# Attention denominators inverted in place and spread over partitions through DRAM, in a new instruction order

## The chip, the cores and the metric

The kernel runs on one core of a Trainium2 chip, as one launch. The core's engines run side by side, each through its own instruction queue in order, and meet at semaphores: TensorE (PE, matmul), VectorE (DVE), ScalarE (ACT), GpSimd (POOL) and SyncE (SP), which here only issues DMAs. SBUF is the on-chip memory, PSUM holds matmul results, DRAM is off chip. The metric is device time in microseconds (us), lower is better.

## What is computed

For x of 4 x 2048 rows of 256 numbers the kernel computes `x + s * silu(g)`, where both branches read the same layer norm xn of x. Cut to what matters here, per batch b, with 16 heads of 64:

```
Q = elu(xn @ Wq + bq) + 1;  K = elu(xn @ Wk + bk) + 1;  v = xn @ Wv + bv
KV = einsum('bshd,bshm->bhdm', K, v)
Z = 1 / (einsum('bshd,bhd->bsh', Q, K.sum(axis=1)) + 1e-6)
o = einsum('bshd,bhdm,bsh->bshm', Q, KV, Z);   attn_out = o @ Wo + bo
x1 = layer_norm(xn + attn_out);  s = layer_norm(x1 + gelu(x1 @ W1 + b1) @ W2 + b2)
g = fp4_linear(silu(fp4_linear(xn, w_gate)) * fp4_linear(xn, w_up), w_down)
```

`fp4_linear` rounds both operands in blocks of 16 to a grid of 4-bit numbers before it multiplies. All is float32; a product is made of three matmuls on a high and a low part of each operand (`mm3`, lines 74 to 77).

## The kernel before

The rows are 64 tiles of 128 (`NT`), in 16 groups of 512 rows (`NG`). A first stage, up to about 520 us, makes the layer norm, the K sums (`ksB`) and, for each batch, the maps `Mh`, `Ml` = KV times Wo. The second stage, which the change concerns, goes through the groups. Nothing is scheduled automatically: for each engine the order is written out by hand, a loop over groups whose body lists steps of this group and of the ones around it. Each step first waits on semaphores. In a group the tiles are a, b, c, d.

The steps that the text below speaks of:

- `q_proj(g,j)` (PE, 6 matmuls of 512 columns into the bank QH), `q_exp` (ACT) and `q_elu` (DVE, L1584) make Q for two heads at a time, j = 0 to 7, as `Q32[:, j, :]` with features on the partitions and 512 rows in the free dimension.
- The denominators. `den_sums` (PE, L676) multiplies `ksB` with Q: 8 matmuls of 512 columns, four of which write different 32-partition strips of the bank AC. `den_copy` (ACT, L1169) takes them to `dn_s`, `den_turn` (PE, L685) transposes them, `den_inverse` (DVE, L1715 to L1723) adds 1e-6, inverts and splits into a high and a low part, `z_turn` (PE, L692) transposes back, `z_copy` (ACT, L1174) stores `zs`, and eight `z_spread` (PE, L704) copy one row of `zs` to the 64 partitions of its head with a selecting matrix `sel`, into QH.
- `z_mul(g,j)` (DVE, L1729) multiplies `Q32[:, j, :]`, in SBUF, with the bank in PSUM that `z_spread` wrote. `z_hi` (ACT, L1088) and `z_lo` (DVE, L1738) split the product, and `at_step(g,j)` (PE, 12 matmuls of 256 columns into AC) adds its part to the attention output.
- `ln1_add`, `ln1_stats` and `ln1_norm` (DVE, L1670 to L1689) are the first layer norm, with `ln1_rstd` on POOL (L2006). `turn_x1` (PE, L739) transposes the result, `h_proj`, `gelu` and `f_step` are the two MLP products.
- The second branch: `gate_up(i,hf)` (PE, 12 matmuls of 352 columns, into GU or QH), `gate_tanh` and `gate_mul` (ACT, DVE L1598 and L1600), `h_max` and `h_scale` (DVE), `h_in` (POOL L1985), `h_abs` (ACT), `h_round` (DVE L1610 and L1612), `h_out` (POOL L1990), `turn_h` (PE L787), `h_hi` and `h_lo` (ACT, DVE L1590), `down(i)` (PE, 18 matmuls of 256 columns into the bank DN), `g_tanh` and `g_mul` (ACT, DVE L1649). `turn_xq` (PE L647), `xq_hi`, `xq_lo`, and `x_in`, `x_out`, `x_round` prepare its input.
- The end of a group on POOL: `x2_affine` (two instructions, L2031 and L2033), `final_mul` (L2038); for the next group `x_plus_bo` (L1980); for the first layer norm `x1_residual` (L2023, L2026). Each of these is one instruction of 128 x 1024 numbers from SBUF to SBUF. `final_add` (DVE, L1748) ends a group.

Of the kernel before, what the change touches and what calls it, by code (L numbers as in the profile page):

```python
# [26 lines left out]
GU_PLACE = {(0, 1): 0, (0, 0): 1, (1, 0): 2, (3, 0): 3, (2, 0): 4, (3, 1): 5}  # L27
GQ_PLACE = {(1, 1): 0, (2, 1): 1}
# [68 lines left out]
def build(nc, src, Wq, bq, Wk, bk, Wv, bv, Wo, bo, W1, b1, W2, b2, g1, be1, g2, be2,  # L97
# [8 lines left out]
    with ctx:
# [151 lines left out]
        def end_of_a(w):  # L258
# [7 lines left out]
            w.wait_ge(S["A_ks"], 5 * NB)  # L266
# [45 lines left out]
        def _(e):  # L312
# [23 lines left out]
            for i in range(NT + 2):  # L336
# [64 lines left out]
            w.wait_ge(S["A_ks"], 5 * b + 5)  # L401
# [50 lines left out]
        def _(e):  # L452
# [95 lines left out]
            def kv_map(b, hf):  # L548
# [4 lines left out]
                w.wait_ge(S["A_ks"], 5 * b + 1)  # L553
# [126 lines left out]
            def den_turn(g):  # L680
                w.wait_ge(S["dc"], g + 1)
                if g:
                    w.wait_ge(S["lnb"], 12 * (g - 1) + 2)
                for t in range(4):
                    last = e.transpose(AC[:, 512 + t * 128:512 + (t + 1) * 128], dn_s[:, t * 128:(t + 1) * 128], ident[:])  # L685
                last.then_inc(S["dt"], 1)

            def z_turn(g):
                w.wait_ge(S["zi"], 4 * g + 4)
                w.wait_ge(S["dc"], g + 1)  # L690
                for t in range(4):
                    last = e.transpose(AC[0:32, t * 128:(t + 1) * 128], f(zhl[:, t, :]), ident[:])  # L692
                last.then_inc(S["zt"], 1)

            def z_spread(g, j):
                w.wait_ge(S["zc"], g + 1)
                w.wait_ge(S["sel"], 8)
                if j >= 2:
                    w.wait_ge(S["zh"], 8 * g + j - 1)
                    w.wait_ge(S["zl"], 8 * g + j - 1)  # L700
                else:

                    w.wait_ge(S["hh"], hh_done(4 * g + 2, 1))
                e.matmul(QH[:, (j % 2) * 512:(j % 2 + 1) * 512], sel[:, j, :], zs[:], start=True, stop=True).then_inc(S["zs"], 1)  # L704
# [8 lines left out]
            def at_step(g, j):  # L713
# [4 lines left out]
                w.wait_ge(S["zi"], 4 * g + 4)  # L718
                w.wait_ge(S["zc"], g + 1)
# [32 lines left out]
            def gate_up(i, hf):  # L752
# [1350 lines left out]
```

## Time and profile before

| | us |
|---|---|
| median of 3 runs | 1845.88 (1845.14 to 1846.9) |
| the profiled execution: its own time | 1859.51 |
| its span | 1857.4 |
| PE, DVE, ACT, POOL busy in it | 1737.5, 1339.3, 981.1, 705.8 |
| one group of the second stage, `den_sums` to `den_sums` | 82.3 |

The span is the time from first to last instruction in the profiler's record. A busy share is an average over stages. Matmuls overlap in the record: one of 256 columns is shown with 0.28 us, but the next starts 0.12 us later, so PE's time is read from the starts or from the chain of work.

### The profile page before, as it was taken

How to read it: one execution, taken by the hardware profiler on the slowest of the kernel's cores; microseconds unless marked ns; L12 is line 12 of the kernel's file. 1: busy time of each engine (PE TensorE's matmuls, PEld its weight loads, DVE VectorE, ACT ScalarE, POOL GpSimd, SP SyncE). 2: the span in 40 equal slices, each digit the busy share in tenths (PEclk: the TensorE clock that was granted, in tenths of full speed). 3: DMA queues.
4: the chain of work that ended last, by engine and by line, in shares of the span. 5: the costliest groups of instructions: out<-in, count | busy, mean ns of one | idle time of the engine just before them, and what ended most of it. 6: DMA issues, size and time to landing. Idle time of an engine off the chain costs nothing.

```text
span 1857.4 us, 29194 instructions
## 1 busy us (share of the span) xinstructions
PE 1737.5 (94%) x10451; PEld 1502.9 (81%) x10451; DVE 1339.3 (72%) x2703; ACT 981.1 (53%) x1772; POOL 705.8 (38%) x518
## 2 busy tenths in 40 slices
PE   6888999999679999999999999999999999999997
PEld 4666778787558888988888888888888898888886
DVE  5575645645367878787787878778887877878785
ACT  4444555656245554646555464655555465555544
POOL 4443433334123343433434343442434344243434
PEclk9898999999989999999999999999999999999999
DMA  5321222322130010111101010210101021010100
GB/s 170 101 79 53 80 96 62 114 67 95 71 105 1 1 46 1 46 44 51 46 1 46 1 47 18 77 46 1 46 1 46 1 94 47 1 46 1 46 1 23
DMA packets 65941, 89.25 MB, mean 48 GB/s; under 512 B 4211, under 2 KB 50439, under 8 KB 64774
## 3 DMA queue, kind: packets, MB, share of 16 engines
q1 hardware_dynamic: 65798, 87.39, 14.2%
q8 instruction: 84, 1.38, 0.3%
q14 instruction: 59, 0.48, 0.1%
HBM read 53.29 MB, written 34.08 MB: 47 GB/s over the span
## 4 chain that ended last, share of the span: by engine, by line
PE 82%; DVE 9%; issue 3%; DMA 2%; ACT 2%; POOL 1%; SPq 1%; POOLq 0%; DVEq 0%; ACTq 0%
PE QH L75 10%; PE QH L77 10%; PE QH L76 10%; PE AC L75 8%; PE AC L77 8%; PE AC L76 8%; PE GU L75 4%; PE GU L76 4%; PE GU L77 4%; PE QH L704 2%; PE TT L787 2%; PE DN L75 2%; PE DN L76 2%; PE DN L77 2%; PE AC L676 2%
## 5 line engine op out<-in xcount | busy, mean ns | idle before, releaser
L1985 POOL TENSOR_TENSOR hb<-hb,rs_h 128x704 f32<-128x704 f32 x64 | 89.0, 1390 | 421.9 <-DVE rs_h L1607 421.9
L1088 ACT ACTIVATE rh<-QH 128x512 fp32r<-128x512 f32 x256 | 152.9, 597 | 107.3 <-DVE QH L1729 104.6
L1744 DVE TENSOR_TENSOR rl<-QH,rh 128x512 fp32r<-128x512 f32 x128 | 87.4, 683 | 99.5 <-ACT rh L1088 93.9
L1359 DVE SCALAR_TENSOR_TENSOR u<-ex,QH 128x512 f32<-128x512 f32 x128 | 84.9, 682 | 91.2 <-ACT ex L956 90.8
L75 PE MATMUL AC<-Mh,rh 128*128 128x256 f32 x512 | 150.6, 294 | 0.0
L75 PE MATMUL AC<-w2h,rh 128*128 128x256 f32 x512 | 144.8, 283 | 0.0
L76 PE MATMUL AC<-w2l,rh 128*128 128x256 f32 x512 | 143.6, 280 | 0.0
L77 PE MATMUL AC<-w2h,rl 128*128 128x256 f32 x512 | 143.6, 280 | 0.0
L77 PE MATMUL AC<-Mh,rl 128*128 128x256 f32 x512 | 143.5, 280 | 0.0
L76 PE MATMUL AC<-Ml,rh 128*128 128x256 f32 x512 | 143.5, 280 | 0.0
L1114 ACT ACTIVATE hqh<-TT 128x384 fp32r<-128x384 f32 x128 | 62.6, 489 | 147.0 <-PE TT L787 147.0
L1990 POOL TENSOR_TENSOR hb<-hb,sn_h 128x704 f32<-128x704 f32 x64 | 89.0, 1391 | 131.7 <-DVE hb L1612 131.7
L1101 ACT ACTIVATE QH<-QH,cols 128x512 f32<-128x512 f32 x128 | 84.6, 661 | 83.5 <-PE QH L77 81.8
L75 PE MATMUL GU<-wgh,xqh 128*128 128x352 f32 x384 | 128.5, 335 | 0.2 <-DVE xql L1658 0.2
L956 ACT ACTIVATE ex<-QH,neg 128x512 f32<-128x512 f32 x128 | 85.7, 685 | 74.8 <-PE QH L77 73.9
L76 PE MATMUL GU<-wgl,xqh 128*128 128x352 f32 x384 | 124.2, 323 | 0.0
L77 PE MATMUL GU<-wgh,xql 128*128 128x352 f32 x384 | 123.7, 322 | 0.0
L75 PE MATMUL QH<-xnTh,wqh 128*128 128x512 f32 x256 | 105.8, 413 | 17.6 <-DMA xnTl<-xt_scratch 17.2
L75 PE MATMUL QH<-wkh,xth 128*128 128x512 f32 x256 | 111.3, 435 | 10.8 <-DVE u L1359 8.0
L1584 DVE SCALAR_TENSOR_TENSOR Q<-QH,eg 128x512 f32<-128x512 f32 x128 | 86.5, 686 | 37.9 <-ACT QH L1085 37.0
L75 PEld LDWEIGHTS AC<-Mh,rh 128*128 128x128 f32 x512 | 97.2, 190 | 17.6 <-issue 17.6
L1083 ACT ACTIVATE eg<-QH 128x512 f32<-128x512 f32 x128 | 76.6, 599 | 65.7 <-PE QH L77 64.8
(233 smaller groups left out, 5805.3 us busy)
## 6 DMA issues: line engine op xcount, KB each, us to landing
xa<-in_L_attn_src SPq DMA_DIRECT2D x16, 512.0 KB, 4.5
xt_scratch<-xth SPq DMA_DIRECT2D x32, 256.0 KB, 4.6
xt_scratch<-xtl SPq DMA_DIRECT2D x32, 256.0 KB, 4.7
xb<-in_L_attn_src SPq DMA_DIRECT2D x16, 512.0 KB, 4.0
xnTh<-xt_scratch SPq DMA_DIRECT2D x32, 256.0 KB, 4.6
xnTl<-xt_scratch SPq DMA_DIRECT2D x32, 256.0 KB, 5.6
out<-x SPq DMA_DIRECT2D x16, 512.0 KB, 6.6
m_scratch<-mh SPq DMA_DIRECT2D x16, 256.0 KB, 2.4
```

The lines of the kernel that those rows point to most:

```text
L75: e.matmul(outp, lh, rh, start=start, stop=False, skip_group_check=check)
L76: e.matmul(outp, lh, rl, start=False, stop=False, skip_group_check=check)
L77: return e.matmul(outp, ll, rh, start=False, stop=stop, skip_group_check=check)
L956: e.activation(Ex[:, c:c + 512], QH[:, c:c + 512], ACT.Exp, bias=neg1[:, 0:1]).then_inc(S["A_e"], 1)
L1083: e.activation(EG[j % 2][:], q_bank(j), ACT.Relu).then_inc(S["qr"], 1)
L1088: e.activation(RH[j % 4][:], src, ACT.Copy).then_inc(S[sem], 1)
L1101: e.activation(q_bank(j), q_bank(j), ACT.Gelu, bias=b1c[:, j:j + 1]).then_inc(S["ge"], 1)
L1359: e.scalar_tensor_tensor(U[i % 2][:, c:c + 512], Ex[:, c:c + 512], 1.0, QH[:, c:c + 512], ALU.min, ALU.max).then_inc(S["A_K"], 1)
L1584: e.scalar_tensor_tensor(Q32[:, j, :], bank, 1.0, r[:], ALU.min, ALU.add).then_inc(S["Q"], 1)
L1744: e.tensor_tensor(RL[j % 4][:], QH[:, (j % 2) * 512:(j % 2 + 1) * 512], f(RH[j % 4][:]), ALU.subtract).then_inc(S["gel"], 1)
L1985: e.tensor_tensor(hb, hb, spread(rs_h[i % 2][:], 44), ALU.mult).then_inc(S["hin"], 1)
L1990: e.tensor_tensor(hb, hb, spread(sn_h[i % 2][:], 44), ALU.mult).then_inc(S["hout"], 1)
```

## The change

1. `den_sums` writes to the free half of the bank DN (columns 256 to 383), one 32-partition strip for each tile of 128 rows: 32 matmuls of 128 columns instead of 8 of 512. It waits for `g_mul` of the group before, tile c, and `down(d)` waits until `den_inverse` has read the strip.
2. `den_inverse` is two DVE instructions over 128 x 128: add from DN into `dn_s`, then a reciprocal in SBUF.
3. `spread_z`, new, on SP: one DMA writes `dn_s` (64 KB) to DRAM. When that has landed, eight DMAs of 256 KB read it back, each giving 64 partitions copies of two rows. They fill `zb_a` and `zb_b` (SBUF, 16 KB on each partition together).
4. `z_mul` reads `Q32` and `zb`, both in SBUF, and writes QH.
5. `den_copy`, `den_turn`, `z_turn`, `z_copy`, `z_spread`, `sel`, `zs`, `zhl` are gone. ACT loses two instructions a group, PE sixteen matmuls.
6. Every engine has a new written order. The bank QH now serves `gate_up(b,0)` alone of the gate products; a group's second stage is moved against the next group's start, so that `down(d)`, `turn_h(d,·)`, `gate_up(b,·)` lie behind `den_sums`.

The core of the diff:

```diff
             def den_sums(g):
                 w.wait_ge(S["Q"], 8 * g + 8)
                 w.wait_ge(S["mld"], 48 * (g // 4 + 1))
-                if g:
-                    w.wait_ge(S["lnb"], 12 * (g - 1) + 1)
-                for half in range(2):
-                    for c in range(4):
-                        j = 4 * half + c
-                        last = e.matmul(AC[c * 32:(c + 1) * 32, 0:512], ksB[:, j * 32:(j + 1) * 32], Q32[:, j, :],
+                w.wait_ge(S["gb"], 4 * g - 1)
+                for j in range(8):
+                    for t in range(4):
+                        last = e.matmul(DN[t * 32:(t + 1) * 32, 256:384], ksB[:, j * 32:(j + 1) * 32], Q32[:, j, t * 128:(t + 1) * 128],
...
             def den_inverse(g):
+                w.wait_ge(S["dn"], g + 1)
+                w.wait_ge(S["zst"], 16 * g)
+                e.tensor_scalar(dn_s[:], DN[:, 256:384], DEN_EPS, None, ALU.add).then_inc(S["zi"], 1)
+                w.wait_ge(S["zi"], 2 * g + 1)
+                e.reciprocal(dn_s[:], dn_s[:]).then_inc(S["zi"], 1)
...
+            def spread_z(g):
+                zd = z_dram[g % 2]
+                w.wait_ge(S["zi"], 2 * g + 2)
...
+                e.dma_start(zd.rearrange("r (c n) -> c r n", c=4), dn_s[:]).then_inc(S["zst"], 16)
+                w.wait_ge(S["zst"], 16 * (g + 1))
+                for k in range(4):
+                    w.wait_ge(S["zq"], 8 * (g - 1) + 2 * k + 2)
+                    if k >= 2:
+                        w.wait_ge(S["h"], 8 * g)
+                    part = (zb_a, zb_b)[k // 2][:, 2 * (k % 2):2 * (k % 2) + 2, :]
+                    for half in range(2):
+                        rows = zd[4 * k + half:4 * k + half + 3:2, :]
+                        e.dma_start(part[64 * half:64 * half + 64], rows.unsqueeze(0).broadcast_to([64, 2, 512])).then_inc(S[f"zb{k}"], 16)
...
             def z_mul(g, j):
                 bank = QH[:, (j % 2) * 512:(j % 2 + 1) * 512]
-                w.wait_ge(S["zs"], 8 * g + j + 1)
+                w.wait_ge(S[f"zb{j // 2}"], 32 * (g + 1))
...
-                e.tensor_tensor(bank, Q32[:, j, :], bank, ALU.mult).then_inc(S["zq"], 1)
+                e.tensor_tensor(bank, Q32[:, j, :], zb(j), ALU.mult).then_inc(S["zq"], 1)
```

The new order is read at three places. First DVE in the middle of a group, from `den_inverse` to the sixth `z_mul`. Before, with `den_inverse` in the first two of the rows shown (the last of its four instructions and the gate product behind it):

```order
L1723 TENSOR_TENSOR zhl<-AC,zhl 128x4x16
L1598 SCALAR_TENSOR_TENSOR hb0<-hb0,QH 128x352
L1600 TENSOR_TENSOR hb0<-hb0,QH 128x352
L1617 TENSOR_REDUCE am_h1<-hb2 128x44
L1729 TENSOR_TENSOR QH<-Q32,QH 128x512 x2
L1738 TENSOR_TENSOR rl0<-QH,rh0 128x512
L1738 TENSOR_TENSOR rl1<-QH,rh1 128x512
L1729 TENSOR_TENSOR QH<-Q32,QH 128x512 x2
L1738 TENSOR_TENSOR rl2<-QH,rh2 128x512
L1738 TENSOR_TENSOR rl3<-QH,rh3 128x512
```

In the change, at the same place, from the reciprocal on (the gate products of tile b stand in the rows left out):

```order
L1778 RECIPROCAL dn_s<-dn_s 128x128
L1650 TENSOR_TENSOR hql<-TT,hqh 128x384
L1670 SCALAR_TENSOR_TENSOR hb1<-hc,hb1 128x704
L1672 SCALAR_TENSOR_TENSOR hb1<-hc,hb1 128x704
```

```order
L1719 TENSOR_TENSOR xql<-TT,xqh 128x512
L1791 TENSOR_TENSOR QH<-Q32,zb_a 128x512
L1677 TENSOR_REDUCE am_h1<-hb2 128x44
L1800 TENSOR_TENSOR rl0<-QH,rh0 128x512
L1791 TENSOR_TENSOR QH<-Q32,zb_a 128x512
L1658 SCALAR_TENSOR_TENSOR hb0<-hb0,GU 128x352
L1660 TENSOR_TENSOR hb0<-hb0,GU 128x352
L1800 TENSOR_TENSOR rl1<-QH,rh1 128x512
L1791 TENSOR_TENSOR QH<-Q32,zb_a 128x512 x2
L1709 SCALAR_TENSOR_TENSOR Gb<-Gb,DN 128x256
L1800 TENSOR_TENSOR rl2<-QH,rh2 128x512
L1800 TENSOR_TENSOR rl3<-QH,rh3 128x512
```

`h_lo(d,1)`, `h_round(a)`, both gate products of tile b and `xq_lo` now stand behind `den_inverse`, ahead of the first `z_mul`; `h_max(b)`, one gate product of tile c and `g_mul(d)` stand among the `z_mul`.

Second POOL, from the input scaling of a tile to the end of the group before. Before:

```order
L1985 TENSOR_TENSOR hb2<-hb2,rs_h1 128x704
L2031 TENSOR_TENSOR x11<-x11,v_g2 128x1024
L2033 TENSOR_TENSOR x11<-x11,v_be2 128x1024
L1990 TENSOR_TENSOR hb2<-hb2,sn_h1 128x704
L2006 TENSOR_TENSOR rsblna<-vtlna,nhalf 128x2 x2
L2038 TENSOR_TENSOR x11<-Gb,x11 128x1024
```

In the change:

```order
L2108 TENSOR_TENSOR hb1<-hb1,sn_h0 128x704
L2149 TENSOR_TENSOR x11<-x11,v_g2 128x1024
L2151 TENSOR_TENSOR x11<-x11,v_be2 128x1024
L2156 TENSOR_TENSOR x11<-Gb,x11 128x1024
L2098 TENSOR_TENSOR x10<-XN,v_bo 128x1024
L2103 TENSOR_TENSOR hb2<-hb2,rs_h1 128x704
L2108 TENSOR_TENSOR hb2<-hb2,sn_h1 128x704
L2124 TENSOR_TENSOR rsblna<-vtlna,nhalf 128x2 x2
```

`x2_affine`, `final_mul` and `x_plus_bo` now stand in a row between `h_out(a)` and `h_in(b)`.

Third PE at the denominators. Before:

```order
L676 MATMUL AC<-Q32,ksB 32x512 x8
L685 MATMUL AC<-ident,eg0 128x128 x4
L75 MATMUL QH<-wgh,xqh 128x352
```

In the change:

```order
L79 MATMUL DN<-wdh,hql 128x256
L794 MATMUL TT<-ident,hb1 128x128 x3
L710 MATMUL DN<-Q32,ksB 32x128 x32
L794 MATMUL TT<-ident,hb1 128x128 x3
L77 MATMUL QH<-wgh,xqh 128x352
```

`den_sums` now follows `down(c)` and `turn_h(d,0)`; behind it stand `turn_h(d,1)`, `gate_up(b,0)`, `gate_up(b,1)`, `turn_xq`, `down(d)`, `gate_up(c,1)`, `turn_h(a,0)` and only then the first `at_step`.

## Rows read from the trace of the kernel before

**Rows 1.** The page: span, busy time of each engine, chain that ended last.

```profile
PE 1737.5 (94%) x10451; PEld 1502.9 (81%) x10451; DVE 1339.3 (72%) x2703; ACT 981.1 (53%) x1772; POOL 705.8 (38%) x518
...
PE 82%; DVE 9%; issue 3%; DMA 2%; ACT 2%; POOL 1%; SPq 1%; POOLq 0%; DVEq 0%; ACTq 0%
```

**Rows 2.** Busy time by stretch of one group: PE, PEld, DVE, ACT, POOL, clock, DMA.

```profile
1038.37:1063.32 24.95, 24.23 (x179) 20.54 (x179) 21.11 (x41) 11.51 (x22) 8.94 (x5) 1.00 0.00 1
1063.32:1070.54 7.22, 5.99 (x44) 5.23 (x43) 6.91 (x20) 1.85 (x4) 3.74 (x3) 1.00 0.00 0
1070.54:1120.66 50.12, 50.12 (x312) 45.38 (x316) 37.99 (x75) 31.91 (x57) 19.50 (x14) 1.00 0.14 43
...
1036.79:1069.42 32.63, 30.82 (x224) 26.37 (x222) 28.48 (x59) 12.86 (x26) 11.79 (x8) 1.00 0.00 1
```

**Rows 3.** Waits of PE in that group: waited for, total, times, longest.

```profile
PE QH L739 <- DVE x L1689: 1.2, 2, 1.0
PE AC L685 <- ACT eg L1169: 0.7, 1, 0.7
```

**Rows 4.** Chain of work in order of time there: start, us, what.

```profile
1038.12 0.16 PE QH L76
...
1038.44 1.90 PE AC L676 x16
...
1041.01 0.66 PE AC L685 x4
...
1043.60 0.44 PE AC L692 x4
...
1045.97 0.66 PE QH L704 x2
```

**Rows 5.** Timeline of DVE in that group: start, us, instruction, idle before.

```profile
1041.10 0.41 DVE L1649 SCALAR_TENSOR_TENSOR Gb<-Gb,DN 128x256 f32<-128x256 f32 x1
...
1041.71 0.23 DVE L1715 TENSOR_SCALAR AC<-AC 128x64 f32<-128x64 f32 x1 [0.20 <-PE AC L685]
1041.97 0.57 DVE L1717 RECIPROCAL AC<-AC 128x64 f32<-128x64 f32 x1
```

**Rows 6.** DMA issues: engine, count, KB each, median us to landing.

```profile
xnTh<-xt_scratch SPq DMA_DIRECT2D x32, 256.0 KB, 4.6
...
m_scratch<-mh SPq DMA_DIRECT2D x16, 256.0 KB, 2.4
...
ks_scratch<-ksA SPq DMA_DIRECT2D x4, 128.0 KB, 1.7
```

**Rows 7.** Issue time of the loads of 256 KB, ns min/median/max.

```profile
L420 SPq DMA_DIRECT2D xnTh<-xt_scratch x32: 371/472/1345, 509.9 to 1734.5; - x32
```

**Rows 8.** DVE with two SBUF inputs: durations, then DVE and POOL timelines.

```profile
L1350 DVE TENSOR_TENSOR kal<-u,kah x32: 673/684/1207, 32.3 to 480.2; 128x512 fp32r<-128x512 f32 x32
...
282.04 1.21 DVE L1350 TENSOR_TENSOR kal<-u,kah 128x512 fp32r<-128x512 f32 x1
...
281.40 1.29 POOL L1902 TENSOR_TENSOR kl<-u,kh 128x512 fp32r<-128x512 f32 x1 [6.75 <-ACT kh L949]
```

**Rows 9.** The same two engines early on, where both ask in turn.

```profile
42.71 2.31 DVE L1309 TENSOR_TENSOR wql<-raw,wqh 128x1024 fp32r<-128x1024 f32 x1
...
43.90 1.71 POOL L1894 TENSOR_TENSOR xnl<-xa,xnh 128x256 fp32r<-128x256 f32 x1
...
44.94 1.75 DVE L1309 TENSOR_TENSOR wql<-raw,wqh 128x1024 fp32r<-128x1024 f32 x1
```

**Rows 10.** Durations of DVE, ns: one SBUF input, the present `z_mul`.

```profile
L1729 DVE TENSOR_TENSOR QH<-Q,QH x120: 689/693/697, 635.1 to 1798.1; 128x512 f32<-128x512 f32 x120
```

**Rows 11.** POOL's long instructions, two groups: total busy, mean ns.

```profile
L2031 POOL TENSOR_TENSOR x<-x,v_g 128x1024 f32<-128x1024 f32 x2 | 4.8, 2398 | 0.0
```

**Rows 12.** The first group: granted clock by stretch, and PE's wait ahead of it.

```profile
552.70:559.50 6.80, 6.80 (x27) 5.72 (x27) 3.88 (x8) 1.57 (x3) 1.39 (x1) 0.50 0.00 0
...
552.64 1.35 PE L704 MATMUL QH<-zs,sel 32*128 32x512 f32 x2 [1.59 <-DVE rl L1738]
```

More of the change, by code:

```diff
@@ L800, in down @@
                 last.then_inc(S["dw"], 1)
+            q_proj(0, 0)
+            q_proj(0, 1)
+            turn_xq(0, 0)
+            q_proj(0, 2)
+            q_proj(0, 3)
+            gate_up(0, 1)
+            q_proj(0, 4)
+            q_proj(0, 5)
+            gate_up(0, 0)
+            q_proj(0, 6)
+            q_proj(0, 7)
+            den_sums(0)
+            gate_up(1, 0)
+            gate_up(1, 1)
+            turn_xq(0, 1)
+            gate_up(2, 1)
+            turn_h(0, 0)
+            at_step(0, 0)
@@ new lines, in _ @@
+            gate_up(2, 0)
+            at_step(0, 1)
+            at_step(0, 2)
+            at_step(0, 3)
+            at_step(0, 4)
+            turn_h(0, 1)
+            at_step(0, 5)
+            at_step(0, 6)
+            at_step(0, 7)
+            down(0)
+            turn_h(1, 0)
+            gate_up(3, 0)
+            turn_h(1, 1)
+            turn_x1(0, 0)
+            turn_x1(0, 1)
+            down(1)
+            h_proj(0, 0)
+            h_proj(0, 1)
+            gate_up(3, 1)
+            h_proj(0, 2)
@@ L1772, in _ @@
             h_max(0)
+            q_elu(0, 6)
             h_scale(0)
-            q_elu(0, 6)
+            q_elu(0, 7)
+            den_inverse(0)
+            h_round(0)
+            gate_mul(1, 0)
+            gate_mul(1, 1)
+            xq_lo(0, 1)
+            z_mul(0, 0)
+            h_max(1)
+            z_lo(0, 0)
+            z_mul(0, 1)
+            gate_mul(2, 1)
+            z_lo(0, 1)
+            z_mul(0, 2)
+            z_mul(0, 3)
+            z_lo(0, 2)
+            z_lo(0, 3)
@@ new lines, in _ @@
+            z_mul(0, 4)
+            z_mul(0, 5)
+            h_lo(0, 0)
+            z_lo(0, 4)
+            z_lo(0, 5)
+            z_mul(0, 6)
+            z_mul(0, 7)
+            h_scale(1)
+            z_lo(0, 6)
+            z_lo(0, 7)
+            gate_mul(2, 0)
+            h_lo(0, 1)
+            h_round(1)
+            ln1_add(0, 0)
+            ln1_stats(0, 0)
+            ln1_add(0, 1)
+            g_mul(0)
+            ln1_stats(0, 1)
+            h_lo(1, 0)
+            ln1_norm(0, 0)
```

712 lines of the change are left out of this document (370 added, 342 removed).

## The prediction

> **What bounds the kernel now.** I read the page first: PE is busy 94% of the span and makes 82% of the chain that ended last [rows 1]. Then the busy times of one group by stretch [rows 2]: with `den_sums` at 1038.37, stretch A to the last `at_step` is 24.95 us, B to the last `gate_up` 7.22, C to the next `den_sums` 50.12, together 82.29, sixteen times. In C PE is busy throughout. In all of it PE truly waits 0.7 us for `den_copy` and 1.2 us for `ln1_norm` [rows 3]. So PE sets the pace; but DVE is busy 21.1 of 24.95 us in A and 6.9 of 7.22 in B, so close behind that I walk through both engines.
>
> **What the change takes from PE.** In the chain [rows 4] `den_turn` is 0.66 us, `z_turn` 0.44, each pair of `z_spread` 0.66, four pairs 2.64: 3.74 us, and the wait of 0.7 for `den_copy`: 4.4 us a group, 71 us in all if nothing else came due. `den_sums` streams the same columns: 8 matmuls of 512 in 1.90 us, four strips at once; now 32 of 128. I take 2.0. Ends: 1.7 (only the columns), and 7.6 (the four strips no longer overlap). The row is the same operation with the same strips, so I stay near the low end.
>
> **What it puts on DVE's path.** Let T be the time since `den_sums` began. In the new order DVE does, from `den_inverse` to the end of `ln1_norm`, the work that it did before between 1036.79 and 1069.42, 28.48 us busy [rows 2], and one `h_lo` (0.5, for 384 columns against the 0.41 for 256 in [rows 5]) more. `den_inverse` stays at about 1.25 us: the add is 0.23 and the reciprocal 0.57 for 64 numbers [rows 5], which I take as 0.3 and 0.95 for 128, and two short steps of 0.22 are gone. `z_mul` stays at 0.69 [rows 10]. Sum 29.0, with 0.7 for the times at which DVE waits for ACT. From T=2.0 it ends at 31.7; then the last `turn_x1` and `h_lo(b,1)` (0.5) and `down(b)` (2.1) bring `h_proj(0)` to T=34.2. PE's own work there is 32.3: a matmul of 352 columns moves the chain by 0.16 [rows 4], one of 256 by its columns by 0.117, so five `gate_up` of 1.95, three `down` of 2.1, eight `at_step` of 1.4, with 2.0 for `den_sums` and 3.0 for the transposes (0.11 a matmul, as in the 0.44 of four). So DVE sets this stretch, and 1.9 us of PE's saving is lost. In the rest PE keeps C's 50.1 less what moved out (`down(b)`, `gate_up(b,·)`, `turn_xq`, `turn_h(d,1)`: 6.8), and gets two waits: `den_sums` must now wait for `g_tanh(c)` and `g_mul(c)` behind `down(c)` (about 0.4 each, for `g_mul` [rows 5], less 0.33 under `turn_h(d,0)`, with latencies 0.6), and a `q_proj` waits 0.3 for `q_elu`. That gives 44.2. The group would be 34.2 + 44.2 = 78.4 us, 3.9 less than now.
>
> **The DMA round trip.** Its cost is bounded by near rows [rows 6, 7]. Here a write of 128 KB to DRAM lands in 1.7 us; each load of 256 KB occupies SP 0.47 us, and 256 KB land in 2.4 us alone and in 4.6 behind 512 KB. `z_mul(0)` needs the write and two loads: 1.7 + 0.5 + 2.4 and 0.3 of semaphores, 4.9; ends 4.4 and 6.9. Both ends are with nothing else in the queue, since `load_xn`, `load_xb` and the store stand behind. `den_inverse` ends at T=3.3, so the copies are there at 8.2 (up to 10.2). What hides them on DVE: `h_lo(d,1)`, `h_round(a)`, both products of tile b and `xq_lo`, to 8.4; on PE two `gate_up`, `turn_xq`, `down(d)`, another `gate_up`, to 11.1. The six later loads follow at 0.47 us each and are needed 4 us apart: hidden. SP waits for the write, and behind it are queued only loads for the next group and the store, both hidden. In the likeliest case the round trip costs nothing, and without its cover all of 4.9.
>
> **A wait that the diff doesn't show.** Today `z_mul` has one input in SBUF and one in PSUM; it runs at 689 to 697 ns whatever POOL does [rows 10]. The change gives it two inputs in SBUF. The trace has such DVE instructions. `kal<-u,kah` takes 0.68, but 1.21 where it is issued at 282.04 while POOL has an instruction from 281.40 to 282.69: it ends 0.68 after 282.57, which is where POOL ends by its record less 0.1 [rows 8]. So it waits for POOL's whole instruction. The other way round, `xnl` of POOL is issued at 43.90 and ends at 45.61, after DVE's two-input instruction ended at 45.02; the next DVE instruction of that kind, right behind, waits in its turn [rows 9]. So they alternate. The page "SBUF — State Buffer" of the Trainium skill, section "Who interferes with whom", states it as a rule: a DVE instruction with two SBUF inputs contends with a GpSimd instruction that reads SBUF, and the second one blocks fully. The trace agrees with it (0.53 us there); by it this change would lose time at `z_mul`, and without it I would forecast 1783 us.
>
> What it does here: POOL does `h_out(a)` when `h_round(a)` is done (T=5.8), then the two of `x2_affine`, 2.40 us each by record, 2.27 real [rows 11]: the first from 7.2 to 9.5. `z_mul(0)`, ready at 8.4, waits 1.1. The second, blocked until 10.1, runs to 12.4; `z_mul(1)`, ready at 11.5, waits 0.9. `final_mul` needs `g_mul(d)`, which stands right behind `z_mul(3)`: 16.2 to 18.5; `z_mul(4)` waits 1.1. `x_plus_bo` gets in behind it and holds up `z_mul(5)` for 2.25. Sum 5.3 us on the engine that sets this stretch, of which 5.15 reach `h_proj(0)`. The group is then 78.4 + 5.15 = 83.55: 1.25 more than now, 20 us in all.
>
> **The clock.** These waits leave PE idle in one piece of 2.95 us, before the fifth `at_step`. In the first group of the trace a wait of 1.59 us stands ahead of 6.8 us at half the granted clock (1.2 instead of 2.4 GHz) [rows 12]; the 1.2 us of idle time in each later group leave it at full. So the clock may fall in part of the groups; a part of it is hidden, since DVE sets the pace. I take 0.4 us a group, 6 in all; ends 0 and 3 us a group (48).
>
> **Rivals.** (1) POOL doesn't get in the way (the lock doesn't hold where DVE writes to PSUM, or POOL's four instructions fall between the `z_mul`). For it: DVE instructions with one SBUF input are untouched. Against: the read side is what `kal` shares with `z_mul`. Then 3.9 us a group are gained: 1846 - 62 = 1783. (2) Slower by much: the clock falls in each group. [...] 1846 + 16 x 4.25 = 1914. (3) Slower by the round trip: copies after T=9.6 let the second `x2_affine` in ahead of `z_mul(0)`, which then starts at 11.9; this costs 1.4 more, and each further microsecond another one. At 10.2: 1846 + 16 x 2.65 = 1888; with strips that no longer overlap in `den_sums` (5.6 us later) 1846 + 16 x 5 = 1926 or so. (4) Gain and waits cancel: my waits are 1.25 a group too high, 1846. (5) That the spreading isn't done as said I exclude: the instruction list has the nine DMAs and no `z_spread`.
>
> **How the numbers follow.** The sum against the profiled execution: 1859.5 + 20 + 6 = 1885.5. That execution is 13.6 us above the median of the runs; against the median it is 1872. Chances: my forecast (port waits, clock mostly held) 0.58, of which 0.13 with waits so much shorter that a gain remains (down to 1820); rival 1 0.17; rival 2 0.12; rival 3 0.08; rival 4 0.05. The likeliest case alone has 1835 to 1900. The range over all goes from 1800, where most of rival 1 (1783) is left out, to 1915, which takes in rival 2. What a measurement of this kernel can tell from no change is about 0.2%, 3.7 us: faster 0.30, same 0.07, slower 0.63.
>
> **What would show it.** In the profile after: no L685, L692, L704; 32 matmuls in `den_sums` within 2 us; `z_mul` with a mean well over 0.69 (four of eight at 1.6 to 2.9, mean near 1.35); POOL's `x2_affine`, `final_mul` and `x_plus_bo` overlapping them, some of these recorded with over 2.4; PE idle before the first, second and fifth `at_step`, with DVE's `rl` as the releaser; a group of 83 to 84 us. The copies landed before `z_mul(0)` is issued. Wrong: `z_mul` at 0.69 throughout beside a running POOL; DVE waiting for `zb`; a `den_sums` of over 3 us; granted clock under 1 in every group.

## The result, and the profile after

The changed kernel takes 1883.59 us (median of 4 runs, 1879.07 to 1884.48) where the kernel before takes 1846.39 (4 runs): a ratio of 1.0197, 95% interval 1.0179 to 1.0215. It is slower, as forecast, by 37 us where 26 were forecast. The profiled execution of the changed kernel took 1884.48 us, its span is 1882.6.

The page of the changed kernel, the lines that answer [rows 1]:

```profile
PE 1702.0 (90%) x10963; PEld 1514.5 (80%) x10963; DVE 1380.5 (73%) x2655; ACT 971.0 (52%) x1740; POOL 712.0 (38%) x518
...
PE 60%; DVE 20%; DMA 8%; issue 6%; ACT 3%; POOL 1%; SPq 1%; DVEq 0%; POOLq 0%; ACTq 0%
```

PE lost 35 us of work, and its share of the chain fell from 82 to 60%; DVE has 20% where it had 9, and DMA 8% where it had 2. The new limit lies on DVE and on the copies.

To see where, I cut one group in two: from the first `den_sums` matmul to the first `h_proj`, and from there to the next `den_sums`. Busy time by stretch (columns as in [rows 2]), first before, then after:

```profile
1038.37:1072.57 34.20, 32.25 (x233) 27.79 (x233) 30.05 (x63) 15.37 (x29) 12.68 (x8) 1.00 0.00 1
1072.57:1120.66 48.09, 48.09 (x302) 43.35 (x304) 35.96 (x72) 29.89 (x54) 19.50 (x14) 1.00 0.14 45
```

```profile
1035.45:1075.86 40.41, 33.74 (x301) 32.12 (x302) 35.55 (x62) 16.20 (x31) 16.25 (x10) 1.00 0.34 81
1075.86:1119.98 44.12, 43.46 (x261) 38.66 (x259) 33.30 (x70) 28.44 (x51) 16.30 (x13) 1.00 0.08 25
```

The second stretch is 44.12 us, against a forecast of 44.2. In the first, PE has 33.7 us of work and stands idle for 6.7 of the 40.4. Over the 15 intervals between one `den_sums` and the next the group is 84.46 us on average where it was 82.45: 30 us more. The part behind the last `den_sums` is 6.7 us longer. Together that is 37 us, the difference of the medians. The two spans differ by 25.2 us only, since the first `den_sums` comes 11.7 us earlier here (530.4 for 542.1), and that isn't owed to the change: the kernel of e6 below has the first stage and the order of the kernel before, and its first `den_sums` is at 531.8. In the profiled execution of the kernel before, the time up to the first `den_sums` was 8 us or more above that in each of the other thirteen profiles (525.3 to 534.4).

The mean also hides a spread. The first interval is 80.1 us, since no group before it has left POOL anything to do there; the fourteen others are 84.5 to 85.8, where those of the kernel before are 82.2 to 82.4 (its own first is 84.9, with the half clock of [rows 12]).

The chain of work through the start of that group, changed kernel (start, us, what), where [rows 4] has `den_turn`, `z_turn` and `z_spread`:

```profile
1035.45 1.99 PE DN L710 x64
1037.46 0.30 DVE dn_s L1776
1037.79 0.96 DVE dn_s L1778
1038.77 2.51 DMA z_scratch<-dn_s
1041.30 0.59 SPq L464
1041.93 4.36 DMA zb_a<-z_scratch
1046.32 1.61 DVE QH L1791
```

`den_sums` takes 1.99 us (x64 counts weight loads and matmuls) and `den_inverse` 1.3 (L1776 and L1778). Then nothing computes on the chain for 7.5 us: the write to DRAM, the issue of the first load, and the landing of the second load of the pair. DVE and POOL in the same place (timeline; start, us, idle time ahead with its releaser):

```profile
1043.27 0.68 DVE L1719 TENSOR_TENSOR xql<-TT,xqh 128x512 fp32r<-128x512 f32 x1
1046.32 1.61 DVE L1791 TENSOR_TENSOR QH<-Q,zb_a 128x512 f32<-128x512 f32 x1 [2.36 <-DMA zb_a<-z_scratch]
...
1049.27 0.69 DVE L1791 TENSOR_TENSOR QH<-Q,zb_a 128x512 f32<-128x512 f32 x1
...
1054.19 4.72 DVE L1791 TENSOR_TENSOR QH<-Q,zb_b 128x512 f32<-128x512 f32 x2
```

```profile
1042.55 2.39 POOL L2149 TENSOR_TENSOR x<-x,v_g 128x1024 f32<-128x1024 f32 x1
1045.01 2.36 POOL L2151 TENSOR_TENSOR x<-x,v_be 128x1024 f32<-128x1024 f32 x1
1053.15 2.42 POOL L2156 TENSOR_TENSOR x<-Gb,x 128x1024 f32<-128x1024 f32 x1 [5.78 <-DVE Gb L1709]
1055.51 2.85 POOL L2098 TENSOR_TENSOR x<-XN,v_bo 128x1024 f32<-128x1024 f32 x1
```

`z_mul(0)` waits 2.36 us for its copies, and then is recorded with 1.61 us where 0.69 is the undisturbed time: POOL's second `x2_affine` runs until 1047.37. A wait of this kind stands inside the recorded duration, not as idle time ahead. `z_mul(1)` meets nothing. `z_mul(4)` and `z_mul(5)` take 4.72 us together instead of 1.29, beside `final_mul` and `x_plus_bo`, the latter recorded with 2.85 where POOL's long instructions have 2.40 in [rows 11], because it too is held. So 2.4 us go to the copies and 0.92 + 3.43 = 4.4 to POOL.

All `z_mul` (ns min/median/max, where [rows 10] has 689/693/697; then idle time ahead of them, times):

```profile
L1791 DVE TENSOR_TENSOR QH<-Q,zb_a x64: 687/690/1871, 541.2 to 1813.9; 128x512 f32<-128x512 f32 x64
L1791 DVE TENSOR_TENSOR QH<-Q,zb_b x64: 680/690/2907, 548.0 to 1823.0; 128x512 f32<-128x512 f32 x64
...
  DMA zb_a<-z_scratch: 37.9, 16
```

What PE waited for in that group (total, times, longest), to set beside [rows 3]:

```profile
PE AC L77 <- ACT rh L1120: 2.9, 1, 2.9
PE AC L77 <- DVE rl L1800: 2.7, 1, 2.7
PE DN L710 <- DVE Gb L1709: 0.7, 1, 0.7
```

The first two are `at_step(0)` and `at_step(4)`. In 13 groups one of them is followed by 3.4 us in which half the clock is granted (1.2 in place of 2.4 GHz), as in [rows 12] and here one group later (columns as in [rows 2]; the clock is the third figure from the end):

```profile
1129.00:1133.40 4.40, 2.15 (x15) 1.90 (x13) 2.55 (x3) 1.18 (x3) 2.85 (x2) 1.00 1.07 222
1133.40:1136.80 3.40, 2.78 (x13) 2.81 (x14) 3.37 (x7) 1.11 (x4) 0.00 (x0) 0.50 1.06 221
```

What it costs depends on where it falls. In ten groups it begins 13.4 to 15.4 us after `den_sums`, behind the first wait; PE is slower then, but has 1.2 to 1.6 us to wait before `at_step(4)` in place of 2.7, and the group takes the same 84.5 us as the two groups in which the clock stays full. In three it begins 25.8 to 26.1 us after `den_sums`, behind the second wait, where nothing hides it: these are the three intervals of 85.6 to 85.8. PE's first wait is alike in all fifteen groups (2.8 or 2.9 us), so its length alone doesn't decide whether the clock falls behind it.

### The profile page after: what moved, and what is told of

Its sections match the earlier page's. It is cut to its first block, busy times and chain, and to the rows that moved or that the text cites. A ratio compares the mean times of both kernels' runs of the same rounds, so it can differ in the third digit from the quotient of the medians.

```text
span 1882.6 us, 30418 instructions
## 1 busy us (share of the span) xinstructions
PE 1702.0 (90%) x10963; PEld 1514.5 (80%) x10963; DVE 1380.5 (73%) x2655; ACT 971.0 (52%) x1740; POOL 712.0 (38%) x518
## 4 chain that ended last, share of the span: by engine, by line
PE 60%; DVE 20%; DMA 8%; issue 6%; ACT 3%; POOL 1%; SPq 1%; DVEq 0%; POOLq 0%; ACTq 0%
PE QH L77 9%; PE QH L79 9%; PE QH L78 9%; DVE QH L1791 6%; PE AC L77 5%; PE AC L78 5%; PE AC L79 5%; DMA zb_a<-z_scratch 4%; PE GU L77 3%; PE GU L78 3%; PE GU L79 3%; DVE rl L1800 2%; DMA z_scratch<-dn_s 2%; PE DN L710 2%; DVE x L1750 2%
## 5 line engine op out<-in xcount | busy, mean ns | idle before, releaser
L77 PE MATMUL GU<-wgh,xqh 128*128 128x352 f32 x448 | 151.6, 338 | 1.9 <-DVE xql L1719 1.9
L1420 DVE SCALAR_TENSOR_TENSOR u<-ex,QH 128x512 f32<-128x512 f32 x128 | 84.9, 682 | 89.6 <-ACT ex L991 89.2
L78 PE MATMUL GU<-wgl,xqh 128*128 128x352 f32 x448 | 148.8, 332 | 0.0
L79 PE MATMUL GU<-wgh,xql 128*128 128x352 f32 x448 | 148.1, 331 | 0.0
L79 PE MATMUL AC<-Mh,rl 128*128 128x256 f32 x512 | 148.0, 289 | 0.0
L78 PE MATMUL AC<-Ml,rh 128*128 128x256 f32 x512 | 147.6, 288 | 0.0
L77 PE MATMUL DN<-wdh,hqh 128*128 128x256 f32 (+1 forms) x384 | 111.4, 290 | 3.2 <-ACT hqh L1146 3.2
L78 PE MATMUL DN<-wdl,hqh 128*128 128x256 f32 (+1 forms) x384 | 108.6, 283 | 0.0
```

What stands on the lines that cost most here:

```text
L77: e.matmul(outp, lh, rh, start=start, stop=False, skip_group_check=check)
L78: e.matmul(outp, lh, rl, start=False, stop=False, skip_group_check=check)
L79: return e.matmul(outp, ll, rh, start=False, stop=stop, skip_group_check=check)
L1420: e.scalar_tensor_tensor(U[i % 2][:, c:c + 512], Ex[:, c:c + 512], 1.0, QH[:, c:c + 512], ALU.min, ALU.max).then_inc(S["A_K"], 1)
```

## The experiments

Two theories. **Two waits on DVE**: the change frees PE, and what it wins is lost because `z_mul` meets POOL at the SBUF (4.4 us a group) and because the copies come late (2.4 us). **Rivals**: `z_mul` is long for another reason (its output in PSUM, or the copies' own traffic); or some other wait of the new order costs it. Times are medians beside runs of the kernel before on the same chip, whose medians were 1848 to 1850. Not all of these kernels compute the result: e1 and e3 leave the denominators out of the product, e2 and e3 load those of the group before, e6 and e9 multiply with other numbers. e4, e5, e7, e8 and e10 to e12 are complete.

**e1: z_mul without a second SBUF input.**

```diff
-                e.tensor_tensor(bank, Q32[:, j, :], zb(j), ALU.mult).then_inc(S["zq"], 1)
+                e.tensor_tensor(bank, Q32[:, j, :], bank, ALU.mult).then_inc(S["zq"], 1)
```

> The changed kernel, but z_mul takes its second input from the PSUM bank that it writes to, not from the copies in SBUF; all waits and all DMAs stay. The denominators are left out of the product. Lock theory (z_mul and a POOL instruction can't read SBUF at the same time): all z_mul last 0.69 us, the 4.4 us of waiting in z_mul 0, 4 and 5 go, the 2.4 us for the copies stay; a group of 84.7 becomes 80.3 and the time 1884 - 16 x 4.3 = 1815. Rival (the long z_mul come from the copies' own DMA traffic into SBUF, or from DVE writing to PSUM): z_mul stays at 1.6 to 2.9 and the time at 1884.

Measured: 1828.79 us, ratio 0.989 (0.986 to 0.992) to the kernel before. All 128 `z_mul`:

```profile
L1791 DVE TENSOR_TENSOR QH<-Q,QH x128: 685/688/697, 543.5 to 1763.2; 128x512 f32<-128x512 f32 x128
```

The copies still land in the same place at the same time, POOL runs the same instructions, and the output is still PSUM. Only the second input has moved, and not one `z_mul` waits. The time is 55 us less than that of the changed kernel; most groups take 80.0 to 80.4. The time is 14 us above what was expected. Half of that are five groups at 81.5 to 81.7: they are the ones in which 3.4 us of half clock follow PE's wait of 1.9 to 2.1 us before `at_step(0)`, which costs 1.5 us a group here. Ten groups wait 1.7 to 2.0 us and keep the clock. Some 4 us more lie in the median, which is that much above the profiled execution.

**e2: copies there in time.** The loads of a group read what the group before has written to DRAM, and are issued ahead of this group's write.

```diff
+                if g:
+                    copies(g, z_dram[(g - 1) % 2])
                 w.wait_ge(S["zi"], 2 * g + 2)
...
                 e.dma_start(zd.rearrange("r (c n) -> c r n", c=4), dn_s[:]).then_inc(S["zst"], 16)
                 w.wait_ge(S["zst"], 16 * (g + 1))
+                if g == 0:
+                    copies(0, zd)
```

> The changed kernel, but the eight loads of a group read the denominators of the group before and are issued ahead of this group's write to DRAM, so that z_mul finds them landed; same DMAs, same bytes. The factors are those of the wrong group. Lock theory: DVE no longer waits 2.4 us for the copies, but z_mul 0, ready at T=8.1, now meets the first instruction of x2_affine (to T=9.4, 1.3 us) and z_mul 1 the second (0.9 us); 5.6 us of lock where 4.4 were. Net 1.1 us a group less: 1866. Rival (the copies alone are the loss): the whole 2.4 us a group come back: 1846.

Measured: 1870.7 us, ratio 1.011 (1.008 to 1.014). DVE's `z_mul` 0, 1, 4 and 5, and POOL's second `x2_affine` (L1796 is `z_mul` here):

```profile
1038.46 1.62 DVE L1796 TENSOR_TENSOR QH<-Q,zb_a 128x512 f32<-128x512 f32 x1
...
1041.42 1.46 DVE L1796 TENSOR_TENSOR QH<-Q,zb_a 128x512 f32<-128x512 f32 x1
...
1047.11 4.71 DVE L1796 TENSOR_TENSOR QH<-Q,zb_b 128x512 f32<-128x512 f32 x2
```

```profile
1039.60 2.72 POOL L2156 TENSOR_TENSOR x<-x,v_be 128x1024 f32<-128x1024 f32 x1
```

This is the case that the prediction had summed: `z_mul` 0, 1, 4 and 5 wait 0.9, 0.8 and 3.4 us, together 5.1. POOL's second instruction is recorded with 2.72 us where it takes 2.36, since it is itself held until `z_mul(0)` ends at 1040.08: the two engines take turns. Of the 2.4 us of DMA wait removed only about 1 us a group is won (83.4 for 84.46), because an earlier `z_mul(0)` runs into two POOL instructions in place of one. The rival's 1846 is excluded.

**e3: both.** The two edits together.

> Both edits: copies loaded early with the data of the group before, and z_mul's second input in PSUM, so that the denominators are left out. If these two waits are all that turned the change into a loss, the group is the 78.4 us of the prediction's sum without them, the time 1783 (between 1775 and 1795). If something else of the new order costs (a wait that I have not seen), it stays above 1800.

Measured: 1787.15 us, ratio 0.965 (0.964 to 0.967). The two stretches of a group:

```profile
1003.91:1037.80 33.89, 33.01 (x302) 31.85 (x302) 31.24 (x62) 16.13 (x31) 15.83 (x10) 1.00 0.11 34
1037.80:1081.94 44.14, 43.45 (x265) 38.69 (x264) 33.33 (x70) 28.51 (x51) 16.37 (x13) 1.00 0.28 72
```

A group is 78.03 us, against the 78.4 of the prediction's sum without the two waits, and the time is 3.5% below the kernel before. PE's waits in the first of these stretches, behind the start of `den_sums`:

```profile
PE QH L752 <- DVE x L1755: 0.5, 2, 0.3
PE TT L799 <- DVE hql L1655: 0.3, 1, 0.3
```

So the new order costs nothing that the sum didn't have; the saving on PE is real, and the two waits are all that hides it. The mean of the 15 intervals is 78.42, since the first takes 83.0, with 10 us at half clock; the others take 78.0 to 78.2.

**e4: the long POOL instructions out of the way.** A complete kernel; order on POOL alone.

```diff
                 if g + 1 < NG:
+                    x_plus_bo(g + 1)
                     h_in(a + 4)
                     x_out(g + 1, 1)
+                x2_scale(g)
+                if g + 1 < NG:
                     h_out(a + 4)
-                x2_affine(g)
+                x2_shift(g)
                 final_mul(g)
                 if g + 1 < NG:
-                    x_plus_bo(g + 1)
                     h_in(b + 4)
```

> The changed kernel, complete, with another order on POOL alone: x_plus_bo ahead of h_in of tile a, the first instruction of x2_affine ahead of h_out(a), the second behind it, final_mul ahead of h_in(b). Lock theory: the long instructions then lie where DVE waits for the copies; only final_mul meets a z_mul (the fifth, 1.25 us). Of the 4.4 us 3.1 go, and a wait of up to 1.5 us moves to h_round(a), hidden in the 2.4 us for the copies: a group of 81.4 to 82.0, 1832 to 1842. Rival (no lock, or h_out(a) late by the instruction ahead of it): no gain, 1884 or more.

Measured: 1832.54 us, ratio 0.990 (0.988 to 0.991): 1% less than the kernel before. DVE, and POOL's first half of `x2_affine`:

```profile
1020.01 2.29 DVE L1670 SCALAR_TENSOR_TENSOR hb<-hc,hb 128x704 f32<-128x704 f32 x1
...
1026.87 0.70 DVE L1791 TENSOR_TENSOR QH<-Q,zb_a 128x512 f32<-128x512 f32 x1 [1.08 <-DMA zb_a<-z_scratch]
...
1033.83 2.52 DVE L1791 TENSOR_TENSOR QH<-Q,zb_b 128x512 f32<-128x512 f32 x2
```

```profile
1019.14 2.41 POOL L2149 TENSOR_TENSOR x<-x,v_g 128x1024 f32<-128x1024 f32 x1 [2.23 <-ACT x L1162]
```

The collision has moved as foreseen: `h_round(a)` (two SBUF inputs, 0.88 us alone) takes 2.29, in time that DVE would otherwise spend waiting for the copies, and of the `z_mul` only the fifth waits, 1.24 us. With the same DMAs and the same instructions, order alone is worth 51 us.

**e5: two moves on DVE.** `h_max(b)` ahead of `z_mul(0)`, `g_mul(d)` behind `z_mul(5)`.

> The kernel of e4_pool_moved, complete, with two moves on DVE: h_max(b) ahead of z_mul 0 (0.87 us of work into the wait for the copies, which is 1.1 to 1.3 us there), and g_mul(d) behind z_mul 5, so that final_mul starts when z_mul 4 and 5 are done and can only meet z_mul 6. Lock theory: 0.9 us from h_max and 0.8 of the 1.25 us at z_mul 4: a group of 79.7 where e4 has 81.4, 1805. Rival (PE sets the pace by now): 1825 or more.

Measured: 1830.27 us, ratio 0.991 (0.989 to 0.993), 25 us above what I expected; a miss. DVE:

```profile
1025.88 0.72 DVE L1791 TENSOR_TENSOR QH<-Q,zb_a 128x512 f32<-128x512 f32 x1 [0.28 <-DMA zb_a<-z_scratch]
1027.34 0.69 DVE L1800 TENSOR_TENSOR rl<-QH,rh 128x512 fp32r<-128x512 f32 x1 [0.73 <-ACT rh L1120]
...
1035.97 2.07 DVE L1791 TENSOR_TENSOR QH<-Q,zb_b 128x512 f32<-128x512 f32 x2
```

`h_max` had not been idle filling: it stood where DVE must wait 0.73 us for `z_hi(0)` on ACT before `z_lo(0)`. Moving it ahead filled one gap and opened the other. And `final_mul` now holds up `z_mul(6)` by 0.8 us in place of `z_mul(4)` by 1.24. So 1.08 and 1.24 us of waiting became 0.28, 0.73 and 0.8, half a microsecond less in the group shown, of which 0.3 reach the mean (81.1 for 81.4).

**e6: the kernel before, with a second SBUF input.** No DMA, no new order.

```diff
-                e.tensor_tensor(bank, Q32[:, j, :], bank, ALU.mult).then_inc(S["zq"], 1)
+                e.tensor_tensor(bank, Q32[:, j, :], Q32[:, (j + 1) % 8, :], ALU.mult).then_inc(S["zq"], 1)
```

> The kernel before, in its own order, with one edit: z_mul's second input is Q32's next tile, in SBUF, instead of the PSUM bank; the denominators are left out of the product. No DMA is added. Lock theory: z_mul 4 meets h_in(b) on POOL (1.2 us), z_mul 5 the first instruction of x2_affine (2.2 us), the others run at 0.69; 3.4 us on DVE, of which some 3 reach the group: 85.3 for 82.3, 1894. Rival (the copies' DMA traffic or the new order is what makes z_mul long): z_mul at 0.69 throughout and 1846.

Measured: 1915.93 us, ratio 1.038 (1.034 to 1.041). DVE's fifth and sixth `z_mul` (L1729), POOL's `h_in(b)` and first `x2_affine`, and the stretch from `den_sums` to `h_proj`:

```profile
1061.79 4.63 DVE L1729 TENSOR_TENSOR QH<-Q 128x512 f32<-128x512 f32 x2 [0.18 <-PE QH L704]
```

```profile
1061.69 1.39 POOL L1985 TENSOR_TENSOR hb<-hb,rs_h 128x704 f32<-128x704 f32 x1 [13.21 <-DVE rs_h L1607]
1063.04 2.82 POOL L2031 TENSOR_TENSOR x<-x,v_g 128x1024 f32<-128x1024 f32 x1
```

```profile
1046.78:1086.51 39.73, 35.54 (x234) 30.50 (x233) 33.38 (x63) 15.37 (x29) 13.39 (x8) 0.91 0.00 1
```

One operand makes the two `z_mul` wait 3.3 us (3.4 expected), in the old order and without any copy in flight: the wait belongs to the pair of operands. Two groups keep the full clock and take 85.0 and 85.1, the 85.3 of the expectation. In the others, the first apart, half the clock is granted behind PE's wait of 2.2 us: the six with 3.4 us of it take 86.6 or 86.7, the six with 6.8 us (one is the stretch shown, 0.91 on average) 87.6 to 88.1. In this kernel PE is the bound, and the clock is not hidden: 1.6 and some 2.8 us. That is the 22 us that the expectation lacks.

**e7, e9: why the copies take 4.4 us.** Both from e4. e7 holds the other six loads until the first two have landed; e9 reads 64 different rows in place of the same two.

```diff
+                    if k == 1:
+                        w.wait_ge(S["zb0"], 32 * (g + 1))
```

```diff
-                        e.dma_start(part[64 * half:64 * half + 64], rows.unsqueeze(0).broadcast_to([64, 2, 512])).then_inc(S[f"zb{k}"], 16)
+                        src_rows = xt_dram[g, half, 0:64, :].rearrange("p (r n) -> p r n", r=2)
+                        e.dma_start(part[64 * half:64 * half + 64], src_rows).then_inc(S[f"zb{k}"], 16)
```

> The kernel of e4_pool_moved, complete, but SP issues the other six loads only when the first two have landed. In e4 the copy that z_mul 0 waits for lands some 4.7 us after the first issue, with six loads behind it. If those six take bandwidth from it, it now lands in about 3 us, z_mul 0 waits for nothing, and the group falls from 81.4 to 80.3 or less. If a queue serves its loads in turn, it lands at the same time and the group stays at 81.4, or rises where z_mul 4 waits for the later ones.

> The kernel of e4_pool_moved, but the eight loads read 64 different rows of 4 KB from another DRAM tensor in place of two rows 64 times; the same count, bytes and destinations, and packets that may be twice as large. The factors of z_mul are left wrong. If reading one row 64 times is what makes the load slow (4.4 us for the pair, where I had taken 2.4 and the issue), z_mul 0 no longer waits and the group falls to 80.3; if it is the bytes over 16 engines and a fixed time, it stays at 81.4.

Measured: 1843.42 (ratio 0.998) and 1835.18 (0.993). The chain of work in e7, then in e9, the landing of the pair:

```profile
1027.19 4.32 DMA zb_a<-z_scratch
```

```profile
1026.00 4.30 DMA zb_a<-xt_scratch
```

Neither the traffic behind the pair nor the repeated rows matter much: over five groups each, the second load lands 3.9 to 4.3 us after its issue when alone, 4.2 to 4.6 in e4 with six behind it, 4.1 to 4.8 with distinct rows. So the six loads behind take some 0.3 us. e7 loses 11 us to e4, and its third `z_mul` now waits some 0.6 us for copies in most groups, where it waits for none in e4. What remains is a fixed time and the bytes: while loads are in flight the changed kernel moves 222 GB/s (the row of 1129.00 above), 2.4 us for the 512 KB of a pair, so some 2 us are fixed (an estimate from these two rows). The loads of 128 KB in e11 land after 2.9 us, 2.3 without the 0.6 of their bytes at that rate.

**e8: the same bytes, cut the other way.** Each load fills all 128 partitions of one copy, from two DRAM rows.

```diff
+                for j in range(8):
...
+                    e.dma_start(zb(j), zd[2 * j:2 * j + 2, :].unsqueeze(1).broadcast_to([2, 64, 512])).then_inc(S[f"zb{j}"], 16)
```

> The kernel of e4_pool_moved, complete, with the same eight loads of 256 KB cut the other way: each fills all 128 partitions of one copy, so z_mul 0 needs one load and not two. If landing time grows with the bytes ahead, the first copy lands 0.6 us earlier by the issue alone and up to 2 us in all; the wait of z_mul 0 (1.1 to 1.3 us) goes: a group of 80.2, 1814. If landing is a fixed time behind the issue, it gains 0.6 us a group at most: 1823.

> The moves of e4 and e5 and the loads of e8 together, a complete kernel. Nothing but z_mul 6 beside final_mul is left of the two waits (0.4 us): a group of 79.2 to 79.5, 1797 to 1803, which is the 78.4 us of the prediction's sum and 1 us. Rival (the gains overlap, since they fill the same wait for the copies): the time of e5, 1805.

(e10 is e5 with the loads of e8.)

Measured: 2331.44 and 2330.2 us, ratio 1.26 both, where 1814 and about 1800 were expected. SP in e8 (four issues), and a stretch in which the loads are in flight (last two figures: DMA share, GB/s):

```profile
1096.13 9.44 SPq L460 DMA_DIRECT2D zb_a<-z_scratch  x4
```

```profile
1099.00:1105.00 6.00, 2.49 (x15) 2.26 (x15) 1.62 (x3) 0.59 (x2) 1.53 (x1) 0.98 0.13 47
```

The DMA engines' mean share is 0.13, two of sixteen, at 47 GB/s where the changed kernel has 1.07 and 222. Later issues block SP for 5.2 us each, and the copies come at that pace. The source pattern has two in its outermost place; in the kernel of the change it is 64. By the Trainium skill, page "DMA: Bandwidth & Descriptors", section "Rules for kernel authors", the number of engines follows from the slowest dimension of the pattern, and a leading dimension of c below 16 confines the whole DMA to at most c engines. The trace agrees: 2/16 = 0.125, read as 0.13. e8 and e10 so say nothing about their own question, whether one load lands sooner than two.

**e11, e12: what the readings are worth together.** e11 goes on from e5: four ACT instructions of the last layer norm between the `q_exp`, `z_mul(0)` and `z_mul(1)` in a row, and the first pair of loads in four of 128 KB with 64 outermost, so that `z_mul(0)` waits for 256 KB. e12 puts `h_max(b)` and `z_lo(0)` between the two `z_mul`.

> A complete kernel that goes on from e5 with three edits. The last layer norm's four ACT instructions go into gaps between the q_exp, so that x2_affine's first half ends before h_round(a) (1.2 us of its 1.4 us wait). z_mul 0 and z_mul 1 stand in a row, so that the 0.7 us in which z_lo 0 waits for z_hi 0 is filled. The pair of loads for z_mul 0 and 1 is cut into four of 128 KB with a semaphore for each of the two, so that z_mul 0 waits for 256 KB and not 512 (1.2 us sooner at the 220 GB/s seen there). From 81.1 a group to 79.1: 1798. If PE is the bound by now it stays above 1815.

> The kernel of e11_best, complete, with h_max(b) back behind z_mul 0 and z_lo 0 ahead of z_mul 1, as in the changed kernel. In e11 z_mul 1 waits 1.3 us for its own copy with nothing in between. If that is right, z_mul 0 waits some 0.7 us more, h_max and z_lo 0 stand in the wait of z_mul 1, and z_lo 0 (0.6 us) is no longer done behind it: a group of 79.2 where e11 has 79.8, 1803. If landing sets both anyway and nothing is gained by the order, it stays at 1812.

Measured: 1812.55 us, ratio 0.980 (0.978 to 0.983), and 1813.44, ratio 0.981 (0.979 to 0.983). Both take 2% less than the kernel before and nearly 4% less than the changed one; 1798 and 1803 had been expected, so both are misses, by 14.6 and 10.4 us. DVE in e11 (L1800 is `z_mul`):

```profile
1022.29 0.70 DVE L1800 TENSOR_TENSOR QH<-Q,zb_a 128x512 f32<-128x512 f32 x1
1024.32 0.70 DVE L1800 TENSOR_TENSOR QH<-Q,zb_a 128x512 f32<-128x512 f32 x1 [1.32 <-DMA zb_a<-z_scratch]
```

`z_mul(0)` no longer waits here (0 to 0.4 us over the fifteen groups behind the first), `z_mul(1)` does, 1.3 us here and 0.1 to 1.3 in the others: the wait was moved by one copy. In both, `final_mul` still holds up `z_mul(6)` by 0.8 us. In e12 DVE waits 0.97 us ahead of `z_mul(0)`, none ahead of `z_mul(1)`, and the group stays at 79.8. Why the third `z_mul`, which comes 0.4 us earlier there, brings nothing at the group's end I have not settled.

| | group, us | time, us | ratio to before |
|---|---|---|---|
| before | 82.5 | 1846 to 1850 | 1 |
| the change | 84.5 | 1883.6 | 1.020 |
| e2, copies early, of the group before | 83.4 | 1870.7 | 1.011 |
| e1, one input in PSUM, no denominators | 80.6 | 1828.8 | 0.989 |
| e3, both, no denominators | 78.4 | 1787.2 | 0.965 |
| e4, POOL's order | 81.4 | 1832.5 | 0.990 |
| e11, orders of POOL, DVE and ACT, smaller first loads | 79.8 | 1812.6 | 0.980 |

(Means over 15 intervals; those of e1 and e3 include the longer ones at half clock.)

## Why the prediction was right, and where not

**PE's saving and the sum without waits: right in size.** 34.2 + 44.2 were forecast for the two stretches, 33.9 + 44.1 measured in e3. Who sets the first stretch is another matter. "So DVE sets this stretch, and 1.9 us of PE's saving is lost": in e3 PE has 33.0 us of work there, not 32.3, and waits 0.9 us for DVE, in three pieces toward the end. The two engines are nearly level, and what DVE takes of the saving is 0.9. `den_sums` takes the 2.0 us that I took from the low end, and its wait for `g_mul(c)` is 0.7 of PE's time where 0.6 was assumed with latencies.

**The wait that the diff doesn't show: right, and by the row that it was read from.** The two-input `kal` [rows 8] gave the rule and the alternation of [rows 9]. `z_mul(4)` and `z_mul(5)` were to wait 1.1 and 2.25, together 3.35; measured 3.43. The place of the first pair was wrong for the changed kernel: `z_mul(0)` waits 0.92 and `z_mul(1)` nothing, 4.4 in all for 5.3, since late copies let POOL pass first; three of eight `z_mul` are long and not four. With the copies in time (e2) it is 5.1 for 5.3. The page "SBUF — State Buffer" of the Trainium skill says the same in its section "Who interferes with whom"; e1 and e6 show it both ways round, by one operand.

**The DMA round trip: the step that failed.** "1.7 + 0.5 + 2.4 and 0.3 of semaphores, 4.9; ends 4.4 and 6.9" came out at 7.5, outside its own ends. The write lands after 2.5 us, not 1.7, though it has half the bytes of the row used [rows 6]. Worse, I priced the pair of loads by 2.4 us, the landing of one 256 KB *write* (`m_scratch<-mh` is one), when a load of that size in the same rows had 4.6; that end I had put down to the bytes ahead of it, and e7 shows 3.9 to 4.3 with nothing behind the pair. So the copies were there at T=10.9 and not 8.2, later than the cover to 8.4, and rival 3 happened as a mechanism: it said that copies after T=9.6 let the second `x2_affine` in ahead and `z_mul(0)` start at 11.9; POOL ends by record at T=11.9 (1047.37 less 1035.45). It was held to have a chance of 0.08. "DVE waiting for `zb`" was one of the prediction's own signs of being wrong, and it came: PE's longest wait, the 2.9 us before `at_step(0)`, belongs to it. What is shown here is a forecast case and a rival together, whose prices overlap: 2.4 us more of DMA, but 0.9 less of waiting for POOL. Of the totals given for them, rival 3's 1888 is nearer to the 1883.6 measured than the forecast's 1872.

**The clock: right in kind.** It falls in 13 groups, hidden in ten; three long groups at about 1.2 us give some 4 us where 6 were taken. The idle piece before `at_step(4)` is 2.7 us where 2.95 were said; the 2.9 us before `at_step(0)`, which most of the falls follow, was not in the sum. So rival 2's condition was nearly met, without its price: 3 us a group need a PE that sets the pace, as in e6, where it cost 1.6 to 3.

**The total.** Against profiled executions, 1885.5 was forecast and 1884.48 measured, but that closeness is luck. A group grew by 2.01 us where 1.65 were forecast, 5.4 us more over 15; the last group and what is behind it grew by 6.7 where I had counted a sixteenth 1.65, 5.1 us more; and the first stage of that one execution of the kernel before was 11.7 us longer, which has nothing to do with the change and took all of it back. The medians are the fair comparison: 1872 forecast, 1883.6 measured, a rise of 37 us where 26 were forecast. In the last group the two waits are paid in full: behind the last `den_sums` e3, without them, takes 78.8 us, the changed kernel 85.3. Even the 2.01 is a mean of one interval that is 4.8 us shorter than before and fourteen that are 2.5 longer on average.

## To carry to other kernels

When an operand moves from PSUM to SBUF, count the DVE instruction's SBUF inputs: with two, each POOL instruction that runs beside it becomes a wait of up to its whole length, so put POOL's long instructions where DVE has none of that kind, which was worth 51 us here. Price a load by a load and for all bytes that the waiter needs, and a trip through DRAM by write and load apart: 2.5 and 0.6 + 4.4 us here. Compare medians with medians: a single profiled execution can carry 10 us that belong to a stage which the change never touched. Filling an engine's wait with the next useful piece of work opens a new one if that piece already covered a latency behind it.

## What I had not expected of the hardware

A 64 KB write of 128 x 128 numbers from SBUF to DRAM lands after 2.46 to 2.56 us in each group looked at, longer than the 1.7 of a 128 KB one [rows 6]. The stretch in which its packets run, in the changed kernel, and the same for the 128 KB write in the kernel before (last two figures: DMA share, GB/s):

```profile
699.59:700.50 0.91, 0.91 (x8) 0.91 (x7) 0.88 (x2) 0.34 (x1) 0.00 (x0) 1.00 0.25 71
```

```profile
183.52:184.03 0.51, 0.51 (x7) 0.51 (x6) 0.51 (x2) 0.51 (x2) 0.00 (x0) 1.00 0.73 257
```

The share is 0.25, four of sixteen, and the write has 4 packets under 512 B at its end where the other has 16. Its pattern in DRAM, `r (c n) -> c r n`, has four in its outermost place, as the loads of e8 had two. So half the bytes take 0.9 us in place of 0.5, and its first packet starts 1.2 us after the issue in place of 0.8. That accounts for the difference, but no run writes the same bytes in another order: that the order is the cause is argued from e8, not shown.

The order of dimensions in a broadcast load decides over a factor of nearly five in rate, 47 GB/s for 222, with SP blocked for 5.2 us at each further issue (e8).

The granted clock isn't settled by the length of PE's wait alone. In e6 PE waits 2.2 us at the same place in each of fifteen groups; two keep the full clock, and thirteen get half of it for 3.4 or 6.8 us.
